# A VectorE polynomial for 42 score banks of the attention of a macaron transformer block

## What is computed

```python
L_q  = exterior(q1, q2)              # 6 numbers a head and token, of length 1
JL_k = exterior(k1, k2) @ _J6.T
attn = jnp.einsum('bqhc,bkhc->bhqk', L_q, JL_k) * 6.0 ** (-0.5)
attn = jnp.where(causal, attn, -jnp.inf)
attn = jax.nn.softmax(attn, axis=-1)                 # 16 heads, causal
out  = jnp.einsum('bhqk,bkhd->bqhd', attn, v).reshape(B, T, D)
return out @ W_o + b_o
```

## Time and profile before

| | |
|---|---|
| three executions | 1233.52, 1239.83, 1246.71 us |
| median | 1239.83 us |
| the profiled execution | 1231.72 us |
| its span, first to last instruction | 1229.9 us |
| TensorE clock granted, mean | 0.963 of 2.4 GHz |
| busy over the span | PE 1055.0 us (86%), ACT 870.1 (71%), DVE 669.0 (54%), POOL 460.7 (37%) |

### The profile page before, as it was taken

How to read it: one execution, slowest core, us unless ns; L and a number is a source line. 1 busy time by engine, 2 the same in 40 slices (tenths; PEclk the granted TensorE clock), 3 DMA queues, 4 the chain that set the end, 5 groups by cost and what they waited for, 6 DMA issues and landing times.

```text
span 1229.9 us, 23939 instructions
## 1 busy us (share of the span) xinstructions
PE 1055.0 (86%) x7557; PEld 572.9 (47%) x7557; DVE 669.0 (54%) x1483; ACT 870.1 (71%) x1243; POOL 460.7 (37%) x675
## 2 busy tenths in 40 slices
PE   8998999958787688988898989888989878876995
PEld 4557888725455122222222222222245768765753
DVE  7896777648798423231334353464578545433544
ACT  4255777624788999999999999999962546654500
POOL 3004555375540425231313234313142564655172
PEclk9999999989999899999999999999999998989997
DMA  9902555443665321010101130201056344544352
GB/s 304 273 2 86 157 156 156 128 131 95 197 197 181 93 66 52 20 51 19 51 22 48 37 102 19 79 18 45 1 176 218 112 142 139 155 125 134 118 162 86
DMA packets 125718, 133.82 MB, mean 109 GB/s; under 512 B 13224, under 2 KB 111888, under 8 KB 125616
## 3 DMA queue, kind: packets, MB, share of 16 engines
q1 hardware_dynamic: 109056, 90.95, 23.3%
q0 software_dynamic: 14448, 39.47, 11.3%
q10 hardware_dynamic: 2112, 2.10, 0.5%
HBM read 80.43 MB, written 52.04 MB: 108 GB/s over the span
## 4 chain that ended last, share of the span: by engine, by line
PE 30%; ACT 22%; issue 15%; DVE 6%; another core or an unknown queue 5%; POOL 1%; DVEq 0%; ACTq 0%; DMA 0%; POOLq 0%
ACT wide L2107 20%; PE banks L2494 8%; PE banks L1991 6%; PE banks L2422 4%; PE banks L2508 4%; PE banks L1965 2%; PE banks L2431 2%; PE banks L2482 2%; DVE x_res L1662 1%; POOL wide L2113 1%; DVE wide L1711 1%; DVE attn_lines_parts L190 1%; PE banks L2005 1%; PE banks L1486 1%
## 5 line engine op out<-in xcount | busy, mean ns | idle before, releaser
L2107 ACT ACTIVATE wide<-banks 128x1536 f32<-128x1536 f32 (+1 forms) x384 | 491.9, 1484 | 5.5 <-PE banks L1965 3.8
L1991 PE MATMUL banks<-wide,attn_attend_v_now 128*32 128x512 f32 (+3 forms) x2560 | 288.0, 541 | 1.7 <-POOL wide L2113 1.6
L2113 POOL TENSOR_SCALAR_AFFINE_SELECT wide<-wide 128x256 f32<-128x256 f32 (+1 forms) x320 | 118.2, 398 | 385.7 <-ACT wide L2107 381.9
L1965 PE MATMUL banks<-attn_attend_q_now,attn_attend_k_now 32*128 32x512 f16 (+3 forms) x1280 | 150.5, 354 | 57.4 <-ACT wide L2107 54.2
L1965 PEld LDWEIGHTS banks<-attn_attend_q_now,attn_attend_k_now 32*128 32x128 f16 x1280 | 38.7, 91 | 292.1 <-ACT wide L2107 245.3
L2494 PE MATMUL banks<-f_xnt 128*128 128x128 f32 x752 | 107.8, 289 | 38.0 <-ACT f_xnt L2583 16.2
L687 POOL DMA_INDIRECT f_region<-xn_rows,f_token_of x79 | 77.6, 982 | 133.0 <-DVE f_token_of L927 79.2
L2494 PEld LDWEIGHTS banks<-f_xnt 128*128 128x128 f32 x752 | 97.4, 202 | 43.2 <-issue 34.5
L2158 DVE COPY sums<-banks 128x512 f32<-128x512 f32 x32 | 22.1, 691 | 162.3 <-PE banks L1991 162.3
L2606 POOL DMA_INDIRECT last_rows_in<-xn_rows,f_spare x72 | 68.8, 956 | 71.4 <-PE banks L2482 29.3
L550 PE MATMUL banks<-f_region,wide 128*128 128x128 f32 x632 | 86.2, 280 | 7.5 <-ACT f_region L655 3.1
(11 more groups left out here) (380 smaller groups left out, 1799.3 us busy)
## 6 DMA issues: line engine op xcount, KB each, us to landing
y_half<-f_xnt SPq DMA_DIRECT2D x94, 128.0 KB
y_slots<-wide SPq DMA_DIRECT2D x79, 128.0 KB
attn_v<-f_more SPq DMA_DIRECT2D x32, 256.0 KB
attn_attend_v_now<-attn_v SPq DMA_DIRECT2D x32, 256.0 KB, 3.4
x_res<-L_attn_x SPq DMA_DIRECT2D x8, 512.0 KB, 7.6
xn_rows<-f_w_all SPq DMA_DIRECT2D x8, 512.0 KB, 4.8
attn_q<-attn_lines_q_out SPq DMA_DIRECT2D x8, 512.0 KB
attn_k<-attn_lines_k_out SPq DMA_DIRECT2D x8, 512.0 KB
```

Of the source, the lines that this page charges most:

```text
L1965: last = pe.matmul(score[i % SLOTS][:, j, column:column + columns(u)], k_now[rows, kt * P:(kt + 1) * P], q_now[rows, qc * QW + c0:(qc + 1) ...
L1991: last = pe.matmul(out_bank[qc][rows, c0:QW], v_now[:, kt, rows], probs[:, place, column:column + columns(u)], start=(kt == 0), stop=(u == ...
L2107: act.activation(probs_flat[:, at:at + width_of[i]], score_flat[i % SLOTS][:, 0:width_of[i]], ACT.Exp, scale=SCALE).then_inc(sem.exp_done, 1)
L2113: pool.affine_select(out=part, in_=part, compare_op=ALU.is_ge, fill=0.0, base=0, pattern=[[0, part.shape[1]], [1, P]], channel_multiplier= ...
```

## The change

42 of the 1152 score banks leave ScalarE. Each is the third bank of a 1536-wide strip off the diagonal. TensorE writes its scores into the free bank instead (`scores_to_raise`, at the end of an earlier step), VectorE evaluates a polynomial in their place, in six instructions, into the same place in `probs` (`raise_scores`), and ScalarE's `ACTIVATE` of that strip is 1024 columns wide. The pairs in `RAISED` are (step at whose end the scores are asked for, strip they belong to). By group: g = 0 seven, 1 seven, 2 nine, 3 seven, 4 five, 5 none, 6 two, 7 five.

The adding of the projections' halves and the raising now go through one loop on VectorE, `between`, in the order of the steps. TensorE gets two new waits: `wait_raised`, until VectorE has read the last asked bank (three of its six instructions), before every further use of the free bank, before a new ask, and before the first unit of a chunk; and in `weigh`, until the bank that this unit needs is raised.

```diff
+RAISED_ONE, RAISED_TWO, RAISED_THREE = ((9, 12), (12, 15)), ((17, 19), (20, 24), (27, 30)), ((33, 37), (36, 39), (40, 44), (43, 46))
+RAISED_LATE = ((35, 38), (39, 44))
+RAISED = ((*RAISED_ONE, RAISED_TWO[-1], *RAISED_THREE), (*RAISED_ONE, *RAISED_TWO, *RAISED_LATE),
+          (*RAISED_ONE, *RAISED_TWO, *RAISED_THREE), (*RAISED_ONE, *RAISED_TWO, *RAISED_LATE),
+          (*RAISED_ONE, *RAISED_TWO), (), RAISED_TWO[1:], (*RAISED_ONE, *RAISED_TWO))
+CURVE_STEPS, CURVE_SCORES_READ = 5, 3
...
     def tensor(pe):
+        asked, projected = [0], [0]
+        def wait_raised():
+            if asked[0]:
+                pe.wait_ge(sem.raise_step, CURVE_STEPS * (asked[0] - 1) + CURVE_SCORES_READ)
+        def scores_to_raise(g, i):
+            strip = raised_at[g][i]
...
+            pe.wait_ge(q_loaded[qc], 16 * (g + 1))
+            pe.wait_ge(kv_loaded[qc], 32 * (g + 1))
+            pe.wait_ge(sem.sums_kept, QC * g + sum(i > pv_step[last_of[qc]] for qc in range(QC - 1)))
+            if projected[0]:
+                pe.wait_ge(sem.proj_added, projected[0])
...
+            wait_raised()
+            pe.matmul(rest_bank(i), k_now[rows, kt * P:(kt + 1) * P], q_now[rows, qc * QW:(qc + 1) * QW], start=True, stop=True
+                      ).then_inc(sem.raise_scored, 1)
+            asked[0] += 1
...
             for j, parts in enumerate(score_banks[WIDE * i:WIDE * (i + 1)]):
+                if j == WIDE - 1 and (g, i) in raised_order:
+                    continue
...
             if kt == 0 and uses > 0:
                 pe.wait_ge(sem.rest_kept, uses)
+            if kt == 0:
+                wait_raised()
             pe.wait_ge(sem.exp_done, N * g + last_strip[u] + 1)
+            if raised_before(g, u):
+                pe.wait_ge(sem.raised, raised_before(g, u))
...
             if before > 0:
                 pe.wait_ge(sem.proj_added, before)
+            wait_raised()
+            projected[0] = before + 1
...
+            if i in raised_at[g]:
+                scores_to_raise(g, i)
...
-                act.activation(probs_flat[:, at:at + width_of[i]], score_flat[i % SLOTS][:, 0:width_of[i]], ACT.Exp, scale=SCALE
+                width = (WIDE - 1) * QW if (g, i) in raised_order else width_of[i]
+                act.activation(probs_flat[:, at:at + width], score_flat[i % SLOTS][:, 0:width], ACT.Exp, scale=SCALE
...
+        def raise_scores(g, i):
+            strip = raised_at[g][i]
+            n = raised_order[g, strip]
+            into, score_of = probs[:, strip % RING * WIDE + WIDE - 1, :], rest_bank(i)
+            dve.wait_ge(sem.pv_done, U * g + held_by[strip - RING] + 1)
+            dve.wait_ge(sem.raise_scored, n + 1)
+            done = CURVE_STEPS * n
+            dve.tensor_copy(into, score_of).then_inc(sem.raise_step, 1)
+            dve.wait_ge(sem.raise_step, done + 1)
+            dve.scalar_tensor_tensor(curve[:], into, CURVE_SHIFTS[0], score_of, ALU.add, ALU.mult).then_inc(sem.raise_step, 1)
+            dve.wait_ge(sem.raise_step, done + 2)
+            dve.scalar_tensor_tensor(into, curve[:], CURVE_SHIFTS[1], score_of, ALU.add, ALU.mult).then_inc(sem.raise_step, 1)
+            dve.wait_ge(sem.raise_step, done + 3)
+            dve.scalar_tensor_tensor(into, into, CURVE_SHIFTS[2], curve[:], ALU.add, ALU.mult).then_inc(sem.raise_step, 1)
+            dve.wait_ge(sem.raise_step, done + 4)
+            dve.scalar_tensor_tensor(into, into, CURVE_SHIFTS[3], curve[:], ALU.add, ALU.mult).then_inc(sem.raise_step, 1)
+            dve.wait_ge(sem.raise_step, done + 5)
+            dve.tensor_scalar(into, into, CURVE_LEAD, 1.0, ALU.mult, ALU.add).then_inc(sem.raised, 1)
+
+        def between(g, first, end, halves, two):
+            for i in range(first, end):
+                if i in halves:
+                    qc, half = halves[i]
+                    add_half(two, qc, half)
+                    if half:
+                        add_up(two, qc)
+                if i in raised_at[g]:
+                    raise_scores(g, i)
...
-                if side == 0 and qc == 1 and later(g):
-                    add(two - 1, QC - 1)
+                if qc < QC - 1:
+                    first, end = ((0, 16), (16, 31), (31, N))[qc]
+                    halves = {i: done for i, done in projections(g, side).items() if first <= i < end and (later(g) or side == 1)}
+                    between(g, first, end, halves, two - 1 if side == 0 else two)
```

More of the change, by code:

```diff
@@ L1792, in attend @@
     shares = sb("shares", [P, QW // HR])
+    curve = sb("curve", [P, QW])
     sums, below, heads = core.sums, core.below, core.heads
@@ L1797, in attend @@
     sem = semaphores(nc, tag, "w_loaded mask_turn stat_turn load_turn scores_ready exp_done masked pv_done sums_kept chain_step holds_ready divided heads_ready "
-                "proj_done proj_added rest_kept stats_done")
+                "proj_done proj_added rest_kept stats_done raise_scored raise_step raised")
     q_loaded, kv_loaded = ring_semaphores(nc, f"{tag}_q_loaded", QC), ring_semaphores(nc, f"{tag}_kv_loaded", QC)
@@ L1851, in attend, with raised_before @@
     assert pv_step[last_of[1]] < 18 and pv_step[last_of[2] + 1] > 25
+    raised_at = [dict(pairs) for pairs in RAISED]
+    raised_order = {(g, strip): n for n, (g, strip) in enumerate((g, strip) for g in range(ALL) for strip in raised_at[g].values())}
+    for strips in raised_at:
+        for i, strip in strips.items():
+            (u, _, _), = score_banks[WIDE * strip + WIDE - 1]
+            assert u not in diagonal and first_column(u) == 0 and pv_step[held_by[strip - RING]] <= i < strip
+    def raised_before(g, u):
+        return max([raised_order[g, strip_of[u, h]] + 1 for h in range(HG) if (g, strip_of[u, h]) in raised_order
+                    and place_of[u, h][0] % WIDE == WIDE - 1] + [0])
     def rested(g, i):
@@ L2280, in group @@
                     routing.statistics(dve, 0, HT)
-                if side == 1 and qc in (1, 2):
-                    for done in ((0,) if qc == 1 else (1, 2)):
-                        add(two, done)
-                        if g == GATE + 3:
-                            dve.wait_ge(sem.stats_done, 3 * QC - 3 + done)
-                            routing.statistics(dve, HT + done * BT, BT)
+                if g == GATE + 3 and qc == 1:
+                    dve.wait_ge(sem.stats_done, 3 * QC - 3)
+                    routing.statistics(dve, HT, BT)
         dve.tensor_reduce(holds[:, 0:1], core.ident[:].rearrange("p (j r) -> p j r", r=HR)[:, :, 0:DH], mybir.AxisListType.XY, ALU.add)
```

9 lines of the change are left out of this document (added).

## The result

| | before | after |
|---|---|---|
| median of four executions | 1243.27 us (1233.52 to 1247.80) | 1269.93 us (1267.22 to 1270.41) |
| the profiled execution | 1231.72 us | 1270.32 us |
| attention, first to last exponential | 407.05 to 904.61, 497.6 us | 412.94 to 939.18, 526.2 us |
| TensorE clock granted, mean | 0.963 | 0.950 |

The ratio is 1.0221, with an interval of 1.0152 to 1.0289. The kernel is slower, as forecast, but by about 27 us and not by 14.5, and 1269.93 lies above the range.

The account below looks back on a forecast made before the run. ScalarE sets the attention's pace, with TensorE 89% busy. Lateness +19.8, group 6's projection +1.1 and TensorE's asks +2.5, less 8.9 of savings, give +14.5 us: median 1254, range 1230 to 1264.

Parts of the forecast that it names:

- that rival: TensorE's clock falls at its stalls in five groups, up to 4 us more each: +20 to +34.5, 1260 to 1274; chance 0.09.
- the place: Unit 16 through step 22's projection to the scores of strip 23, where TensorE waits for VectorE, in groups 1, 2, 3, 4, 7.
- the polynomial's SBUF-only steps: VectorE's instructions in a raise without PSUM operands; the two-source ones priced at 0.725 us chained, like those reading PSUM.
- The chain of VectorE: VectorE's queue from chunk 0: raises 9, 12, chunk 1, raise 17; unit 16 starts at +19.75 or +20.85, against +17.3 before.
- R: VectorE's time for raising one bank, six instructions in a row: 4.2 us, bounds 4.1 and 4.35.
- How late the place is: Scores of strip 23 late by 3.3 us in groups 2, 4 and 4.4 in 1, 3, 7: 19.8 us in all.
- What is left of the gain: ScalarE's savings: 21 of 42 banks at 0.425 us stay, 8.9 us; the rest lost at late strips or to TensorE.
- Against it: Evidence against a clock fall: the attention's mean clock was 0.99 before, with TensorE waits of up to 0.95 us.
- What was to show it: Signs in the profile after: ScalarE idle 20 us or more, busy 18 less, TensorE waiting 1 to 2 us before unit 16.
- Clock below 0.97: Sign that the prediction is wrong: TensorE's clock in the attention below 0.97.
- Hidden: VectorE's chain delays nothing before unit 16, needing a raise under 3.4 or 3.1 us: -11.5 us, 1228; chance 0.15.
- Late, but by less: A raise takes 3.7 us, so the five places are 1.8 us less late each, 9 us: +5.5, 1245; chance 0.19.

Follow-up runs that it names:

- the kernel with both edits: Changed kernel with zero products filling TensorE's waits in groups 1, 3, 7 and GpSimd's bias adds cut to 8 columns a block: 1250.66 us, one execution.

## Why the prediction was right in sign and wrong in size

The number was 1254, the range ended at 1264, the median is 1269.93. In the attention +14.5 was forecast and +28.7 came. Two steps of the prediction failed. It put the clock at nothing in its sum, by weighing that rival at 0.09, and the clock took 6.7 us at the place that it had named. And it priced the polynomial's SBUF-only steps like the others, whatever GpSimd does beside them, and that took 3.8 us.

The 28.7 divide like this, by the experiments. 6.7 are the clock's falls at the place in groups 1, 3 and 7. 3.8 are the bias adds in groups 0 and 1. 2.8 are two more falls, ahead of chunk 0 in groups 2 (1.25) and 7 (1.5); the kernel with cut adds and no raises has one too, of 1.5 in group 5, so they aren't put down to the raises. 0.4 lie ahead of chunk 0 in group 0, where the attention's first stretch at low clock ends later. That is 13.7, and 15.0 are left. The last column of the table, less the 2.0 of its fall in group 2, gives 14.3. The mechanism that the prediction priced at 14.5 is worth 14 to 15.

**The chain of VectorE.** Right. Chunk 1 was forecast to start at +12.2 and +12.5, it came at +12.0 and +12.1. Unit 16 was forecast at +19.75 and +20.85, it came at +19.47 and +20.23. R was taken as 4.2 with bounds 4.1 and 4.35; it is 4.0 to 4.1. The term that was too high is the last instruction, taken as 0.57: it takes 453 ns, like the SBUF copy in the earlier trace rows, as the Trainium skill ("VectorE: DVE Perf Modes", the perf-mode tier table) has it. In time the SBUF copy gains less than the "twice the rate" of the prediction: 458 against 691 ns is a factor of 1.5.

**How late the place is.** Too high by a quarter. 3.3 and 4.4 us were forecast, 19.8 in five groups. At unit 21, in the kernel with both edits, which keeps the clock up there, it is late by 2.6 (group 4: +27.76 against +25.17) and 3.35 (group 3: +28.52 against +25.17): 2 x 2.6 + 3 x 3.35 = 15.2. Group 6: 0.9 (+26.09), forecast 1.1.

**What is left of the gain.** Too high, and by nearly as much in the other direction. 8.9 less 2.5 for the asks was forecast, -6.4. The remainder is -1.1 (15.0 - 15.2 - 0.9) to -1.8 (with the 14.3). What was wrong in it: only strips 38, 39 and 46 were given up to TensorE, and only ten asks of 42 were charged. The one-instruction raise shows TensorE's limit in many more places: 42 banks bring 5.3 us, 6 to 7 without its fall of the clock, where 17.9 less ten asks, 2.5, would be 15.4. An ask costs TensorE 0.16 and not 0.25 us, so all 42 would take 6.7; the rest of what is missing are savings at strips where TensorE has no time to spare. The masks (below) took 0.9 in group 0. That the sum comes out right is luck: two errors of some 5 us that cancel, and not evidence that each term was good.

**The clock.** The rival was there, with the right place and the right mechanism, and was given 0.09. It gave 1 to 4 us a group in five groups, +20 to +34.5 in all; the fall came in three groups, at 2.0 to 2.6, and the total is inside its band only with the bias adds in it. What led astray was the step that weighed it. "Against it" stood the waits of up to 0.95 us in the earlier trace rows, single ones, with TensorE at work around them. Here there are 0.82 and 1.41 within 3 us, and 0.65 behind them, and the prediction's own times had TensorE stand for 2.45 us before unit 16 on the even side and 3.55 on the odd (+19.75 and +20.85 against +17.3). The Trainium skill's goals table ("TensorE: Matmul & The Clock Gate", "Why this matters for your kernels") asks for no idle gap over about 3 us. No gap at this place is longer than 1.41 in groups 3 and 7 and 1.67 in group 1, and the clock still fell to 0.50 in all three, while in groups 2 and 4 it held. So the rule passes a case that the trace fails, and it should not have lowered the chance. At waits of that size either can come, and nothing in the rows of before said which; a chance near one half would have been fair.

**GpSimd and VectorE.** Missing altogether, neither a term nor a rival. In groups 0 and 1 GpSimd's bias adds lie beside the raises, 3.8 us. A smaller one is in six groups: the last six of GpSimd's masks for chunk 1, which unit 8 waits for, before and after (group 2):

```profile
545.13 2.14 POOL L2113 TENSOR_SCALAR_AFFINE_SELECT wide<-wide 128x256 f32<-128x256 f32 x6 [0.68 <-ACT wide L2107]
```

```profile
561.60 3.06 POOL L2176 TENSOR_SCALAR_AFFINE_SELECT wide<-wide 128x256 f32<-128x256 f32 x6 [0.71 <-ACT wide L2170]
...
564.80 1.28 PE L2048 MATMUL banks<-wide,attn_attend_v_now 128*32 128x384 f32 x16 [0.87 <-POOL wide L2176]
```

The masks take 0.92 us longer beside raise 9, and the unit that needs them waits 0.87. Without raise 9, or without the SBUF-only steps, they take 2.14 and the wait is gone. ScalarE loses 0.9 to 0.95 us at strips 15 and 16 by it, in groups 0 to 4 and 7: in group 2 strip 16 starts 11.63 us behind chunk 0, and 10.72 without the SBUF-only steps. In five of these groups VectorE's chain sets the time anyway, and it costs nothing more; in group 0 it makes most of the difference between -1.4 forecast and -0.5.

**What was to show it.** ScalarE idle 20 or more: 42.9. Busy time down by 18: by 8.7 only. Strips in a row overlap in the records (1.58 us long, 1.33 apart) and so count less than strips that stand alone; idle and busy time have to be read together, 497.4 before and 526.1 after. TensorE waits before unit 16 for 1 to 2 us: 1.41. Chunk 1 starts late: yes. Group 3 grows: by 6.3; group 0 shrinks: no, +1.6, but without the 1.5 of the bias adds and the 0.4 of the clock at the start it would be -0.3. Clock below 0.97: 0.96. That was the prediction's own sign of being wrong, and it was met.

**Rivals.** "Hidden" fell by unit 16's times. "Late, but by less" took a raise as 3.7 us, and it is 4.0 to 4.1; the place is less late all the same, by 4.6 us of the 9 that it gave, and the total went the other way.

## What to carry to other kernels

Before work moves to an idle engine, ask two things of each place and not of the sums: how many moved pieces stand in that engine's queue between two things that others wait for, and which engine becomes the pace once the relieved one is faster. Here the first turned a gain into +14, and the second left 5 to 7 us of 17.9 even with a nearly free VectorE.

When a change makes TensorE wait several times within a few us, forecast both clocks and give each a real chance; the cheapest test is to fill the waits with products of zeros. And when VectorE gets instructions with two SBUF sources, look up what GpSimd does in the same microseconds.

## What the runs showed of the hardware

- The clock fell from 1.00 to 0.50 at waits of 0.82 and 1.41 us with work between them (group 3 after), and stayed there for 6.8 us, nearly all of it at full work. The longest wait before any fall at this place was 1.67 us. A fall of 6.8 us cost 2.0 to 2.6 us. Eleven small products in place of the waits kept it at 1.00 in groups 1, 3 and 7 of both kernels that have them.
- In groups 1, 3 and 7 it fell in all three kernels without the filling. In group 2, at one wait of 1.07 to 1.41 us, it fell in three kernels and held in two, with 0.65 us behind it; in group 4, with one of 1.07 to 1.55 and one of 0.65, it held in all five. Without the raises of step 17 it never fell there.
- A float32 `scalar_tensor_tensor` of two SBUF sources took 2.73 us instead of 0.69 beside GpSimd's float32 add, and the add 2.81 instead of 2.38; with one PSUM source the mean of 84 is 687 ns. Six masks of GpSimd took 3.06 us instead of 2.14 beside two such instructions.
- A product of one bank that runs alone takes 0.38 us, and seven of them added 1.1 us to TensorE's busy time where the clock stayed at 1.00, 0.16 each.
